# A conditioned linear-attention layer on one core: the mask term of K moved to VectorE and GpSimd, and a start-up in another order

## The reference, cut to what matters

```python
xn = _ln(x, ln_w, ln_b)
q = xn @ Wq + bq
k = xn @ Wk + bk + (1.0 - src_mask) * -1000000.0
q = softmax(q.reshape(b, t, h, dh), axis=-1)      # over the 32 features of a head
k = softmax(k.reshape(b, t, h, dh), axis=1)       # over the 64 tokens
v = ((xn @ Wv + bv) * src_mask).reshape(b, t, h, dh)
att = einsum('bnhd,bnhl->bhdl', k, v)
y = einsum('bnhd,bhdl->bnhl', q, att).reshape(b, t, d)
emb_out = (silu(emb) @ W_emb + b_emb)[:, None, :]
scale, shift = split(emb_out, 2, axis=2)
hh = _ln(y, ln2_w, ln2_b) * (1.0 + scale) + shift
return x + silu(hh) @ W_out + b_out
```

## Time and profile before

| | before |
|---|---|
| median of 3 runs | 332.36 us (332.33 to 333.7) |
| profiled execution | 333.64 us, span 331.8 us |
| PE busy | 314.4 us (95%) |
| DVE busy | 278.8 us (84%) |
| POOL busy | 198.8 us (60%) |
| ACT busy | 186.0 us (56%) |
| shares of the chain that ended last | PE 85%, DVE 6%, POOL 3%, DMA 2% |

### The profile page before, as it was taken

How to read it: one execution, slowest core, us unless ns; L and a number is a source line. 1 busy time by engine, 2 the same in 40 slices (tenths; PEclk the granted TensorE clock), 3 DMA queues, 4 the chain that set the end, 5 groups by cost and what they waited for, 6 DMA issues and landing times.

```text
span 331.8 us, 14388 instructions
## 1 busy us (share of the span) xinstructions
PE 314.4 (95%) x5644; PEld 269.4 (81%) x5644; DVE 278.8 (84%) x749; ACT 186.0 (56%) x360; POOL 198.8 (60%) x261
## 2 busy tenths in 40 slices
PE   3999999999999999999999999999999999998646
PEld 2487788988889898989888898989898898988645
DVE  4697789989897979899897979798898979786771
ACT  1428375565674847555656748465556657454340
POOL 2305238757666866757676768767576767657610
PEclk9999999999999999999999999999999999999777
DMA  7702100040404030130404040211204010201021
GB/s 249 250 0 66 53 15 4 4 129 2 128 5 126 0 96 30 44 82 0 126 0 126 0 126 0 73 54 35 92 0 126 0 63 0 66 4 65 2 66 63
DMA packets 19418, 19.68 MB, mean 59 GB/s; under 512 B 817, under 2 KB 18865, under 8 KB 19394
## 3 DMA queue, kind: packets, MB, share of 16 engines
q1 hardware_dynamic: 18144, 17.96, 17.4%
q10 hardware_dynamic: 1250, 1.39, 1.2%
HBM read 10.95 MB, written 8.39 MB: 58 GB/s over the span
## 4 chain that ended last, share of the span: by engine, by line
PE 85%; DVE 6%; POOL 3%; DMA 2%; issue 1%; ACT 1%; SPq 0%; POOLq 0%; DVEq 0%
PE bv L674 30%; PE bk L674 27%; PE by L674 13%; PE by L744 4%; PE bv L733 4%; PE by L776 4%; PE by L724 3%; DMA q_t<-in_wv 2%; DVE q_s L557 1%; DVE ystat L647 1%; DVE y_s L640 1%; POOL h_lo L243 1%; DVE xt_lo L578 1%; DVE qmax L552 1%; POOL y_s L350 1%
## 5 line engine op out<-in xcount | busy, mean ns | idle before, releaser
L239 POOL TENSOR_TENSOR z_s<-z_s,mod_shift 128x512 f32<-128x512 f32 x30 | 30.7, 1046 | 41.4 <-DVE z_s L565 41.4
L408 ACT ACTIVATE k_t<-k_t 128x512 f32<-128x512 f32 x32 | 20.2, 631 | 41.5 <-DVE k_t L591 41.5
L243 POOL TENSOR_TENSOR h_lo<-h_s,h_hi 128x512 fp32r<-128x512 f32 x30 | 38.1, 1295 | 5.7 <-ACT h_hi L434 4.7
L674 PE MATMUL bv<-w_o_hi,h_hi 128*128 128x256 f32 x128 | 35.3, 297 | 4.5 <-ACT h_hi L434 4.5
L358 POOL TENSOR_TENSOR x_all<-x_all,bo_all 128x1024 f32 (+1 forms) x16 | 38.6, 2411 | 0.0
L391 ACT ACTIVATE xt_hi<-by 128x512 fp32r<-128x512 f32 x32 | 17.5, 595 | 36.8 <-PE by L744 36.8
L587 DVE TENSOR_REDUCE kmax<-bk 128x8 f32<-128x512 f32 x32 | 22.1, 691 | 16.6 <-PE bk L674 16.1
L350 POOL TENSOR_SCALAR y_s<-y_s,yr 128x256 f32<-128x256 f32 x62 | 34.0, 563 | 2.6 <-POOL yr L347 2.2
L674 PE MATMUL bv<-w_o_lo,h_hi 128*128 128x256 f32 x128 | 35.0, 294 | 0.0
L440 ACT ACTIVATE xhat<-x_all,xr 128x256 f32 (+1 forms) x64 | 33.1, 591 | 2.6 <-POOL xr L333 2.6
L345 POOL TENSOR_TENSOR yr<-yr,neg_half 128x4 f32<-128x4 f32 x16 | 16.2, 1014 | 30.4 <-DVE yr L654 30.4
(11 more groups left out here) (106 smaller groups left out, 840.1 us busy)
## 6 DMA issues: line engine op xcount, KB each, us to landing
x_all<-in_x SPq DMA_DIRECT2D x16, 512.0 KB, 4.3
out<-x_all SPq DMA_DIRECT2D x15, 512.0 KB, 3.2
z_s<-in_w_emb ACTq DMA_DIRECT2D x1, 512.0 KB, 8.4
h_s<-in_w_emb ACTq DMA_DIRECT2D x1, 512.0 KB, 10.0
out<-x_all SPq DMA_DIRECT2D x2, 256.0 KB, 2.1
y_s<-in_wk SPq DMA_DIRECT2D x1, 256.0 KB, 3.0
q_t<-in_wq SPq DMA_DIRECT2D x1, 256.0 KB, 5.0
th<-in_cond_t ACTq DMA_DIRECT2D x1, 256.0 KB, 6.7
```

The costliest lines, as they stand in the source:

```text
L239: return eng.tensor_tensor(z, z, mod_shift[:, c, span(g, GB)].unsqueeze(2).broadcast_to([P, GB, SEQ]), ALU.add)
L243: return eng.tensor_tensor(h_lo[:, c, :], h_s[:, c, :], h_hi[:, c, :].bitcast(fp32), ALU.subtract)
L408: nc.scalar.activation(k_t[:, par, c, :], k_t[:, par, c, :], ACT.Exp).then_inc(kexp_d, 1)
L674: return nc.tensor.matmul(dst, lhsT, rhs, start=start, stop=stop)
```

## The change

**The mask term of K.** `n_all`, `pick` and `sel` go, with the first product of each K half. SP loads for each group the 512 mask values of its sequences into all 128 partitions of `off` (`load_off`). ACT turns them into 1 - mask in place (`mask_offset`), for group i+1 at the end of step i. DVE adds -1000000 times that to K's product on its way from PSUM to `k_t` (`kadd_d`), and takes the maximum out of `k_t`. The subtraction of the maximum moves to POOL (`k_shifted`), K0 at the head of its step, K1 behind `h_low`. ACT's exponential of K1 moves behind the value copies of tiles 2 and 3. PE now waits for each half of `xt_hi` on its own.

**The start-up.** x of group 0 comes first, in halves; w_k moves to ACT's queue, behind the small vectors. DVE takes the statistics of each half as it comes, works out the last two columns of `xr` and makes `xhat` of tiles 2 and 3 itself. PE runs eight dummy products ahead of K's bias products and eight behind; the bias products of q and v move behind K's products of step 0. The tanh of cond moves into step 0, the weights of q, v and w_out and the modulation on DVE behind the statistics of group 1.

```diff
@@ sync
-            sp.dma_start(w_k, ...).then_inc(wk_in, 16)
-            load_x(0, 0)
+            def load_off(g, parity):
+                sp.dma_start(off[:, parity, :].unsqueeze(1),
+                             mask_g[span(g, 1)].unsqueeze(0).broadcast_to([P, 1, GT])).then_inc(off_in[parity], 16)
+            for n in range(2):
+                sp.dma_start(x_all[:, 0, 2 * n * D:2 * n * D + 2 * D].rearrange("p (t d) -> p t d", d=D),
+                             x_h[0][:, 2 * n:2 * n + 2, :]).then_inc(x_first[n], 16)
...
+            load_off(0, 0)
+            load_x(1, 1)
...
                     load_x(i + 1, 1 - par)
+                    wait(sp, kadd_d, 2 * i)
+                    load_off(i + 1, 1 - par)
@@ gpsimd
-            def select(g, parity):
-                wait(pool, k_d, 2 * g - 2)
-                nc.gpsimd.tensor_copy(sel[:, parity, :], pick[:, span(g, 1)].broadcast_to([P, P])).then_inc(sel_d, 1)
+            def k_shifted(g, parity, c):
+                wait(pool, kmax_d, 2 * g + c + 1)
+                kk = k_t[:, parity, c, :].rearrange("p (b s) -> p b s", s=SEQ)
+                nc.gpsimd.tensor_tensor(kk, kk, kmax[:, c, :].unsqueeze(2).broadcast_to([P, GB, SEQ]),
+                                        ALU.subtract).then_inc(ksub_d, 1)
             def body(i, par, N, F, B, O):
+                if F:
+                    k_shifted(i, par, 0)
...
+                if F:
+                    k_shifted(i, par, 1)
@@ scalar
             act.dma_start(small[:, :], columns_in).then_inc(small_in, 16)
+            act.dma_start(w_k, ...).then_inc(wk_in, 16)
...
+            def mask_offset(g, parity):
+                wait(act, off_in[parity], 16 * (g // 2 + 1) if isinstance(g, int) else 8 * (g - parity) + 16)
+                nc.scalar.activation(off[:, parity, :], off[:, parity, :], ACT.Identity, scale=-1.0,
+                                     bias=1.0).then_inc(off_d, 1)
...
                     v_tile(i, par, 3)
+                    wait(act, ksub_d, 2 * i + 2)
+                    nc.scalar.activation(k_t[:, par, 1, :], k_t[:, par, 1, :], ACT.Exp).then_inc(kexp_d, 1)
+                if N and not (isinstance(i, int) and i < 0):
+                    mask_offset(i + 1, 1 - par)
@@ vector
                         wait(dve, k_d, 2 * i + c + 1)
-                        wait(dve, ksub_d, 2 * i + c - 1)
-                        kk = bk_[c][:, :].rearrange("p (b s) -> p b s", s=SEQ)
-                        nc.vector.tensor_reduce(out=kmax[:, c, :], in_=kk, axis=AX.X, op=ALU.max).then_inc(kmax_d, 1)
-                        wait(dve, kmax_d, 2 * i + c + 1)
+                        wait(dve, off_d, i + 1)
...
-                        nc.vector.tensor_tensor(k_t[:, par, c, :]..., kk, kmax..., ALU.subtract).then_inc(ksub_d, 1)
+                        nc.vector.scalar_tensor_tensor(k_t[:, par, c, :], off[:, par, :], -1000000.0, bk_[c][:, :],
+                                                       ALU.mult, ALU.add).then_inc(kadd_d, 1)
+                        wait(dve, kadd_d, 2 * i + c + 1)
+                        wait(dve, ksub_d, 2 * i + c - 1)
+                        nc.vector.tensor_reduce(out=kmax[:, c, :], in_=k_t[:, par, c, :]..., axis=AX.X,
+                                                op=ALU.max).then_inc(kmax_d, 1)
@@ tensor
+            def warm(n):
+                for _ in range(n):
+                    mm(be[0][:, 0:P], ident[:, :], ident[:, :], True, True)
             pe.wait_ge(pool_init, 3)
+            warm(8)
...
             beta(bk_[0], w_k, 2 * D, D)
-            pe.wait_ge(wqv_in, 32)
-            beta(bv_[0], w_qv, 0, 2 * D)
+            warm(8)
...
-                        mm(bk_[c][:, :], sel[:, par, :], n_all[:, :], True, False)
-                        wait(pe, hi_d, 2 * i + 2)
                         for j in range(C):
-                            mm(bk_[c][:, :], w_k_hi[:, j, out_c], xt_hi[:, j, :], False, False)
+                            wait(pe, hi_d, 2 * i + j + 1)
+                            mm(bk_[c][:, :], w_k_hi[:, j, out_c], xt_hi[:, j, :], j == 0, False)
...
                     if isinstance(i, int) and i == 0:
+                        pe.wait_ge(wqv_in, 32)
+                        beta(bv_[0], w_qv, 0, 2 * D)
                         emb_products()
-                        pe.wait_ge(weights_ready, 3)
+                        pe.wait_ge(weights_ready, 2)
```

More of the change, by code:

```diff
@@ L405, in body @@
                 if F:
-                    for c in range(C):
-                        wait(act, ksub_d, 2 * i + c + 1)
-                        nc.scalar.activation(k_t[:, par, c, :], k_t[:, par, c, :], ACT.Exp).then_inc(kexp_d, 1)
+                    wait(act, ksub_d, 2 * i + 1)
+                    nc.scalar.activation(k_t[:, par, 0, :], k_t[:, par, 0, :], ACT.Exp).then_inc(kexp_d, 1)
                 if B:
@@ L438, in body @@
                     wait(act, xt_d, 2 * g - 2)
-                    for t in range(T):
+                    for t in range(T) if not (isinstance(g, int) and g == 0) else (0, 1):
                         nc.scalar.activation(xhat[:, 1 - par, t, :],
@@ L470, in x_stats @@
                 first = isinstance(g, int)
-                wait(dve, x_in[parity], 16 * (g // 2 + 1) if first else 8 * (g - parity) + 16)
+                if first and g == 0:
+                    dve.wait_ge(x_first[0], 16)
+                elif first:
+                    wait(dve, x_in[parity], 16 * (g // 2 + parity))
+                else:
+                    wait(dve, x_in[parity], 8 * (g - parity) + 16 * parity)
                 wait(dve, xr_d, 4 * g)
                 for t in range(T):
+                    if first and g == 0 and t == 2:
+                        dve.wait_ge(x_first[1], 16)
                     nc.vector.bn_stats(xstat[:, t, :], group_of(x_all, g)[:, :, t * D:t * D + D]
@@ L478, in x_stats, with first_xhat, fold_rows @@
                     nc.vector.bn_aggr(xmv[:, t, :], xstat[:, t, :]).then_inc(xmv_d, 1)
-            def fold_and_mask():
+            def first_xhat():
+                dve.wait_ge(xr_d, 2)
+                nc.vector.tensor_tensor(xr[:, 2, :], xmv[:, :, 0], xr[:, 1, :], ALU.mult).then_inc(xr_d, 1)
+                dve.wait_ge(xr_d, 3)
+                nc.vector.tensor_scalar(xr[:, 3, :], xr[:, 2, :], -1.0, 1.0, ALU.mult, ALU.add).then_inc(xr_d, 1)
+                dve.wait_ge(xr_d, 4)
+                for t in (2, 3):
+                    nc.vector.tensor_scalar(xhat[:, 0, t, :], x_all[:, 0, t * D:t * D + D], xr[:, 1, t:t + 1],
+                                            xr[:, 3, t:t + 1], ALU.mult, ALU.add).then_inc(xhat_d, 1)
+            def fold_rows():
+                link(nc.vector.memset(fold[:, :, :], 1.0))
                 dve.wait_ge(small_in, 16)
                 link(nc.vector.tensor_tensor(lnb, lnb, lnw, ALU.subtract))
-                link(nc.vector.memset(fold[:, :, :], 1.0))
                 for c in range(C):
@@ L654, in body @@
                     nc.vector.tensor_scalar(yr[:, 2, :], ymv[:, :, 0], -1.0, None, ALU.mult).then_inc(yve_d, 1)
-                if isinstance(i, int) and i == 0:
-                    modulation()
                 if F:
@@ L705, in qv_tile @@
                 else:
[L706 removed]
+                    wait(pe, kadd_d, 2 * i + t - 1)
                 tok = slice(t * P, t * P + P)
```

90 lines of the change are left out of this document (41 added, 49 removed).

## The result

The changed kernel's median is 331.39 us (329.34 to 332.77, 20 runs) against 333.3 for the kernel before on the same chip (331.94 to 334.43, 20 runs): ratio 0.9945, 95% interval 0.9928 to 0.9962, so 1.9 us faster where 3.35 were forecast. The profiled execution took 331.00 us, span 329.2, which is 2.6 less than the one before.

The account below looks back on a forecast made before the run. PE was taken to bound steps 3 to 15, several engines in turn the start-up. +1.2 at the start and -4.55 over the steps give -3.35, from a median of 332.36 to 329.0 us; range 327.1 to 332.4.

Parts of the forecast that it names:

- The steps: Steps 3 to 15: two mask products leave PE, 18.31 to 17.96 us, 0.35 a step, 4.55 over thirteen.
- Restart (0.57): PE's xt_lo product ahead of K0: after a real wait the next product comes 0.57 later, costing 0.10.
- no wait of DVE's: Bound steps: DVE keeps up, its step of 17.6 being under PE's 17.96 by 0.3.
- the second stretch: From step 2's xt_lo product to step 15's: -4.4, from 0.23 in step 2 and 12 times 0.35.
- The start: Start-up through step 2: PE enters the bound steps 1.2 us later than before, 0.2 without the collision.
- I count POOL's 3.45 in series with DVE: Start-up, shared port: POOL's subtraction (1.05) and addition (2.40) delay DVE in full; step 1's product +1.0.
- ACT's path: Steps 0 and 1: K's second exponential and the mask Identity ahead of xt_hi cost 1.3 each time.
- The end: From step 15's xt_lo product to the last product: only -0.3, what is left of step 15.
- The last two steps keep their operations: End of the run: operations stay the same, so the sum has no term for it.
- The early clock: Part of the first rival (chance 0.2): PE up early, -0.9 from K's bias products; 328.0 to 327.1 us.
- K0's mask product was only cover: Second rival, bound steps: only 0.23 a step gained, 3.0 in all, 330.6 us; chance 0.22.
- POOL holds DVE: Third rival, every step: POOL's new subtraction delays DVE's yr scaling, step 18.6, 337.5 us; chance 0.08.

Follow-up runs that it names:

- tile_64: Changed kernel plus an unused tile of 64 bytes a partition behind neg_half, moving every later tile; 330.95 us, ratio 0.9938.
- pool_held: Changed kernel with POOL's addition of b_out to x in step 0 waiting for the modulation; 331.45 us, ratio 0.9961.
- start_only: Changed kernel's new start-up, with the mask products and exponentials of the kernel before; 335.92 us, ratio 1.0097 to the kernel before.
- mask_only: Changed kernel's new mask path, with the start-up of the kernel before and no dummy products; 329.42 us, ratio 0.9894 to the kernel before.
- dummies_26: Changed kernel with 5 instead of 8 dummy products in the second batch, 6 records fewer; 329.6 us, ratio 0.9917.
- after_again: The changed kernel run once more, unchanged; 331.06 us, ratio 0.9933 to the kernel before.
- no_dummies: Changed kernel without both batches of dummy products; 331.8 us, ratio 0.9961 to the kernel before.

## Why the prediction came out as it did

**The steps: right, with two errors that cancel.** 0.35 a step was forecast, 0.33 came. Restart (0.57), no wait of DVE's, the add at 0.69 and POOL at 1.04 are as written. But at equal placement of the tiles (`tile_64`, 17.92) the products gave 0.39, of which K0's was worth 0.16 instead of 0.12 if K1's brought its whole 0.23; the moved tiles took 0.06 to 0.08 back through the pace of the w_o products, which no row of before could tell. Of the 0.5 by which the second stretch fell short, 0.3 are step 2's: 18.53, with a stop of 0.31 in its att products, against 18.42 before.

**The start: forecast later than it was.** The xt_lo product of step 1 was forecast at 34.7 and came at 33.24, that of step 2 at 50.2 and came at 48.39. Transposes (12.04 against 11.6), the table load (9.59) and the first q/v product (23.81 against 24.05) were close. (The terms written down add to 11.5 for the transposes and 23.8 for the q/v product, not 11.6 and 23.95.) The term that was mis-sized is "I count POOL's 3.45 in series with DVE": the collision is real, but it added 2.8 (0.72 on w_o_hi, 2.09 on w_o_lo), and the rest of DVE's path was shorter too, so xt_lo ended at 33.2 instead of 34.65. Without the collision DVE would have been there that much earlier and would have waited for ACT, as it does in `pool_held`. On ACT's path 1.3 was forecast for its two operations ahead of xt_hi(1); they cost 0.98 (7.32 from the first q/v product to xt_hi, 6.34 before). In step 1 they cost 0.96 once more (xt_hi 13.19 after the xt_lo product, not 13.53), and the product came 1.96 behind xt_hi, where before it was 2.68.

**The end: the step that decided.** The step that failed is "The last two steps keep their operations", from which the sum put the end at nothing. The operations are the same, and the stretch is 1.8 longer: PE's stream crosses a line of instructions three products ahead of the end of the att products, and kv and all that follows wait for the last of them; a second crossing delays the y products. The two stops cost 2.7, of which 0.8 came back. What puts them there is the number of instructions ahead, the 32 records of dummies and the mask products that left: neither `start_only` (dummies and mask products) nor `mask_only` (none of either) has a stop in the att products. That a stop is a wait for instructions is inferred from the packets that land 1.2 to 1.6 ahead of its end in every profile; no run delays a packet by itself. The errors are -1.8 at the start, +0.5 in the steps and +2.1 at the end, which makes the 331.0 of the profiled execution out of the 330.3 forecast. That the total came within 0.7 is luck: the start's error hid the end's. Without the first stop's 1.7 it would have been near 329.3; `dummies_26` took 328.7. The medians, 333.3 and 331.39, lie closer together (1.9) than the two profiled executions (2.6), by as much as single executions of one kernel differ.

**The rivals.** The early clock came in some executions: K's bias products, forecast between 1.4 and 3.2 in all, took 2.6 in the first profile, and their first four records 1.21 in `after_again` against 1.98. It paid nothing there, since the clock fell again in PE's wait for the table load (first q/v product at 24.07 against 23.81). That K0's mask product was only cover is refuted by the steps, that POOL holds DVE by yr's 0.17.

## What to carry to other kernels

In a long unrolled stream of tiny products, instructions ahead of it are part of its timing: look for "issue" gaps with an instruction packet that lands ahead of their end, and if one stands in front of a result that everything waits for, shift the stream by a few instructions until it falls into a wait that is there anyway. When two engines arrive together, an edit on one of them measures nothing; ease both before the idea is dropped. Removing or adding a tile moves all later ones, so measure a change of tiles apart from the change of work.

## What the runs showed of the hardware

- PE stopped for up to 1.72 us without a releaser at fixed products of its stream; 32 product records less ahead of it moved the stop by 31 (`no_dummies`), 6 less moved the second stop by 6 (`dummies_26`). Each stop ended 1.2 to 1.6 us after a packet of 16 KB on the instruction queue had landed (303.53 and 304.99 in the changed kernel); such a packet took 0.9 to 1.8 us.
- The same place in the stream doesn't always stop PE: in `start_only` the packet landed at 305.30, ahead of the att products (307.11), and they had no break.
- 24 products of 256 columns took 2.80, 2.83 or 2.88 us as all tiles behind one lay 96, 64 or 32 bytes past a multiple of 128 (h_hi's place; `tile_64`, `tile_32`, changed kernel). Which operand counts wasn't tried.
- The same program had K's first bias products at 1.98 in one execution and 1.21 in another, though the windows give a granted clock of 1.00 from 5.4 to 7.4 us in both. An idle stretch of PE of some 2 us was followed by a level of 0.59 in `after_again`, and not in the first profile.
